# The mixing of a tree feed-forward on one Trainium2 core: twelve scaled copies of each block against one transposed block and path weights spread by TensorE

## The chip, the cores and the metric

The kernel runs on one core of one Trainium2 chip. The time is device microseconds of one execution; several executions of each kernel were timed, and one more was profiled. PE is TensorE, DVE is VectorE, ACT is ScalarE, POOL is GpSimd, and SP is SyncE, which here only issues DMAs.

## The reference, cut to what matters

The input x has shape 32 x 64 x 64 x 64. A tokenizer with small attention windows reduces it to 32 x 256 tokens of 64 features, a state space layer follows, and then a feed-forward in which each token walks down a binary tree of 8 levels. The change touches the last part and the rows that feed it.

```python
for _ in range(DEPTH + 1):                    # DEPTH = 7
    all_nodes.append(current)
    score = jnp.einsum('td,td->t', flat_x, w1s[current]) + b1s[current]
    all_logits.append(score)
    choice = ((jnp.sign(score) + 1.0) / 2.0).astype(jnp.int32)
    current = current * 2 + choice + 1
logits = jnp.stack(all_logits, axis=1)
path_weights = jax.nn.gelu(jnp.abs(logits), approximate=False)
out = jnp.zeros((T, OUTPUT_WIDTH), dtype=x.dtype)
for i in range(DEPTH + 1):
    nodes_i = all_nodes[i]
    t_i = jnp.einsum('td,tdo->to', flat_x, w2s[nodes_i]) + b2s[nodes_i]
    out = out + t_i * path_weights[:, i][:, None]
```

T is 8192 tokens. w2s holds 255 matrices of 64 x 64. All data is float32.

## The kernel before, in words

The program has three stages, one after the other: `tokenizer`, `scan_and_route` and `mix_blocks`. Between two stages every engine meets the others.

`scan_and_route` walks down the tree for all tokens and sorts them into 32 groups by their node at level 5. For each token it writes one row of `ROW` = 144 floats to DRAM (`rows_by_group`): the normalised token x (64 floats at `X0`), 12 path magnitudes (`P0`: six for levels 0 to 5, two candidates at level 6, four at level 7, zero where the token did not go), the token's h for the residual (64 at `H0`) and its number (`ID0`). POOL writes the rows with indirect DMAs, 8 of 128 rows for each of 8 chunks of 1024 tokens (`scatter`, L944), after computing some of the magnitudes (`path_weights`, L922 to L933).

`mix_blocks` takes the sorted rows in 96 blocks of 128 tokens; all tokens of a block belong to one group and need the same 14 matrices, stored as `wt`: 6 slabs of 128 x 64 (two units each) and a seventh slab with the biases and an identity that adds h. Two blocks, which the kernel calls h = 0 and 1, make a pair; there are 48 pairs.

- SP loads a block of rows into a ring of `ROWS` = 8 (L1579), once the block that lay there has been used.
- ACT applies gelu to the 24 magnitudes of a pair in place (L1630), copies the group's weights to `w_cur` (L1638), copies the four left turned slabs out of PSUM (L1640) and the results into `orow` (L1649), a ring of 8 blocks.
- DVE multiplies x by each of the 12 path weights, which makes `m_xs`, 12 scaled copies of 64 floats per token (L1600). It copies the other turned slabs (L1608) and the mixed result `oT` (L1614).
- PE transposes the 12 copies of a block, two at a time, and the magnitudes with h (L1666, L1671, L1673: 7 transposes a block). It then multiplies the 7 slabs of both blocks by the weights, the blocks in turn on the two column halves of the array (L1684: 14 matmuls, 28 records), and transposes the result back (L1691).
- POOL copies each block's token numbers to `ids` (L1701) and writes the result rows to `out` by indirect DMA (L1710).

Each engine's order is written out by hand. PE in step m turns pair m, mixes pair m - 1 and turns pair m - 2 back; steps of four pairs stand in a hardware loop. Each of `turned`, `mixed_bank` and `back_bank` exists twice in PSUM. So a product is turned back after the next pair's transposes and the next product have gone in between.

## Time and profile before

| | us |
|---|---|
| median of 3 runs | 756.32 |
| lowest, highest | 755.45, 758.33 |
| the profiled execution's own time | 755.77 |
| its span | 753.9 |
| tokenizer, until about | 352 |
| scan_and_route, until about | 545 |
| mix_blocks, from about 545 until its last DMA issue ends | 744.4 |

The profiled execution gives one span for the whole program; a row of the timeline starts with the time from the span's start and the length of the instruction, merged rows say x and a count, and the bracket tells how long the engine was idle before and what ended that. A releaser "remote" is one that the profile does not name. A PE record of a float32 matmul covers half of its passes, so 14 matmuls show as 28. PE's ends are modelled.

### The profile page before, as it was taken

To read this page: it belongs to the slowest core of one execution; us is meant where nothing else is said; L and a number is where in the kernel's file an instruction comes from. 1 tells how busy PE (TensorE), PEld (TensorE's weight loads), DVE (VectorE), ACT (ScalarE), POOL (GpSimd) and SP (SyncE) were. 2 spreads that over 40 slices of the span, in tenths; PEclk is the share of its full clock that TensorE was granted. 3 is DMA by queue.
4 is the path that set the end of the run, shared out by engine and by line. 5 is a ranking of instruction groups with operands and counts; after the bars stand their busy time and mean duration, and the time that the engine had idled before them with its cause. 6 is when DMAs were issued, how large, how long until landed. Compare 5 with 4: busy or idle time off the path is not lost. (4 is left out here: it accounts for less than half of the span.)

```text
span 753.9 us, 17120 instructions
## 1 busy us (share of the span) xinstructions
PE 634.7 (84%) x5322; PEld 333.0 (44%) x5322; DVE 564.2 (75%) x1090; ACT 451.2 (60%) x916; POOL 489.2 (65%) x541
## 2 busy tenths in 40 slices
PE   1699999999999999953799898873089999999990
PEld 1122222222222222211466565542078887887870
DVE  1379888888888889872489898987177777877770
ACT  1587777777777777611587777752055655656560
POOL 5756888888888887466105655557427776767773
PEclk9999999999999999985799999998579999999996
DMA  8033333333333330001776301001122222111200
GB/s 330 14 113 113 112 113 113 113 112 113 113 113 113 113 112 1 2 0 26 121 132 142 132 31 33 32 29 43 34 61 55 55 53 51 53 46 52 55 14 0
DMA packets 49055, 57.71 MB, mean 77 GB/s; under 512 B 31966, under 2 KB 44780, under 8 KB 46882
## 3 DMA queue, kind: packets, MB, share of 16 engines
q1 hardware_dynamic: 43410, 49.98, 22.2%
q0 software_dynamic: 5120, 6.84, 2.9%
q8 instruction: 31, 0.51, 0.3%
q14 instruction: 30, 0.25, 0.1%
q10 hardware_dynamic: 464, 0.13, 0.1%
HBM read 50.02 MB, written 10.28 MB: 80 GB/s over the span
## 5 line engine op out<-in xcount | busy, mean ns | idle before, releaser
L1710 POOL DMA_INDIRECT out<-orow,ids x96 | 100.3, 1044 | 60.0 <-DMA out<-orow,ids 33.5
L629 PE MATMUL b_v<-x_px,w_kv 64*64 64x512 f32 x256 | 133.3, 605 | 0.0
L630 PE MATMUL b_v<-x_px,w_kv 64*64 64x512 f32 x256 | 133.3, 605 | 0.0
L631 PE MATMUL b_k<-x_px,w_kv 64*64 64x512 f32 x256 | 133.3, 605 | 0.0
L628 PE MATMUL b_k<-x_px,w_kv 64*64 64x512 f32 x256 | 133.2, 604 | 0.0
L1600 DVE TENSOR_TENSOR m_xs<-m_rows 128x768 f32<-128x768 f32 x96 | 91.2, 950 | 26.5 <-ACT m_rows L1630 26.0
L399 POOL TENSOR_TENSOR pre<-va 128x1024 f32<-128x1024 f32 x32 | 76.2, 2382 | 41.8 <-DVE va L485 41.8
L944 POOL DMA_INDIRECT rows_by_group<-r_pay,r_slot_i x64 | 71.4, 1116 | 42.4 <-DVE r_slot_i L1295 24.7
L378 POOL TENSOR_TENSOR half_px<-x_px 128x1024 f32<-128x1024 f32 x32 | 75.9, 2372 | 32.3 <-DMA x_px<-in_x 27.0
L485 DVE TENSOR_TENSOR va<-b_a,v_sb 128x512 f32<-128x512 f32 x128 | 84.9, 685 | 12.5 <-PE b_a L646 12.4
L471 DVE TENSOR_TENSOR qk<-b_k,q 128x512 f32<-128x512 f32 x128 | 86.6, 679 | 8.2 <-PE b_k L631 6.8
L328 ACT ACTIVATE v_sb<-b_v 128x512 f32<-128x512 f32 x128 | 75.6, 591 | 24.7 <-PE b_k L631 23.7
L1684 PE MATMUL mixed_bank<-m_xsT,m_w_cur 128*64 128x128 f32 x1344 | 84.3, 276 | 0.8 <-ACT m_xsT L1640 0.8
L238 ACT ACTIVATE x_sq<-x_px 128x1024 f32<-128x1024 f32 x64 | 67.1, 1048 | 19.2 <-PE b_x L679 19.2
L1684 PEld LDWEIGHTS mixed_bank<-m_xsT,m_w_cur 128*64 128x64 f32 x1344 | 72.7, 137 | 9.4 <-issue 7.8
L643 PE MATMUL b_a<-a_sb,e_sw 64*64 64x512 f32 x128 | 68.8, 619 | 9.1 <-DVE va L485 9.1
L646 PE MATMUL b_a<-a_sb,e_sw 64*64 64x512 f32 x128 | 68.9, 619 | 0.0
L644 PE MATMUL b_a<-a_sb,e_sw 64*64 64x512 f32 x128 | 68.9, 619 | 0.0
L645 PE MATMUL b_a<-a_sb,e_sw 64*64 64x512 f32 x128 | 68.9, 619 | 0.0
L1638 ACT ACTIVATE m_w_cur<-wt 128x448 f32 x96 | 55.1, 574 | 18.1 <-issue 16.8
L628 PEld LDWEIGHTS b_k<-x_px,w_kv 64*64 64x64 f32 x256 | 29.0, 132 | 81.2 <-issue 62.0
L1666 PE MATMUL turned0a<-ident,m_xs 128*128 128x128 f32 x192 | 30.9, 285 | 20.7 <-DVE m_xs L1600 18.1
(235 smaller groups left out, 1621.7 us busy)
## 6 DMA issues: line engine op xcount, KB each, us to landing
x_px<-in_x SPq DMA_DIRECT2D x16, 2048.0 KB, 7.8
m_rows<-rows_by_group SPq DMA_DIRECT2D x96, 72.0 KB
wt<-in_w2T SPq DMA_DIRECT2D x8, 512.0 KB
rows_by_group<-rows_by_group SPq DMA_DIRECT2D x1, 2286.0 KB, 12.4
out<-orow,ids POOLq DMA_INDIRECT x96, 2.2
rows_by_group<-r_pay,r_slot_i POOLq DMA_INDIRECT x64
wt<-in_w2T SPq DMA_DIRECT2D x2, 256.0 KB
wt<-in_w2T SPq DMA_DIRECT2D x4, 128.0 KB
```

The costliest lines, as they stand in the source:

```text
L328: a.activation(v_sb[:, t % 2, n, :], b_v[n % 2][:, :], ACT.Copy).then_inc(done["v_copied"], 1)
L378: g.tensor_tensor(half_px[:, s, :, :], v[:, s, 0:2, :], v[:, s, 2:4, :], ALU.add).then_inc(done["px_halved"], 1)
L399: g.tensor_tensor(p1, v[:, :, 0:2, :], v[:, :, 2:4, :], ALU.add).then_inc(done["halved"], 1)
L471: d.tensor_tensor(qk[:, slot(n), :].rearrange("p (h s w) -> p h s w", s=S, w=HW), b_k[n % 2][:, :].rearrange("p (h s w) -> p h s w", s=S, ...
L485: d.tensor_tensor(va[:, slot(n), :], b_a[n % 2][:, :], v_sb[:, t % 2, n, :], ALU.mult).then_inc(done["va_ready"], 1)
L628: mm(b_k[i][LO, :], w_kv[LO, 0, LO], px(t, j, LO), start=True, stop=True)
L629: mm(b_v[i][HI, :], w_kv[LO, 1, LO], px(t, j, LO), start=True, stop=True)
L630: mm(b_v[i][LO, :], w_kv[HI, 1, HI], px(t, j, HI), start=True, stop=True)
L631: mm(b_k[i][HI, :], w_kv[HI, 0, HI], px(t, j, HI), start=True, stop=True).then_inc(done["kv_product"], 1)
L1600: d.tensor_tensor(xs[:, i % RING, :, :], rows[:, i, X0:X0 + C].rearrange("p (o c) -> p o c", o=1).broadcast_to([P, UNITS, C]), rows[:, i, ...
L1684: t = mm(ob[(j + 1) % 2][C * h:C * h + C, 0:P], w_cur[:, i + h, u, :], xsT[:, i + h, u, :], start=u == 0, stop=u == KT - 1)
L1710: nc.gpsimd.indirect_dma_start(out_d, bass.IndirectOffsetOnAxis(ap=ids[:, b % (2 * ROWS):b % (2 * ROWS) + 1], axis=0), orow[:, b % ROWS, : ...
```

## The change

The row becomes 208 floats: x is stored twice side by side (128 floats), so that one transpose of a block puts x on partitions 0 to 63 and again on 64 to 127. POOL makes the second copy once per chunk, ahead of the scatters.

In the mixing x is no longer multiplied before the transpose. ACT writes gelu of the magnitudes as bfloat16 and again as float32; DVE splits off two more bfloat16 parts, so that three parts add up to the float32 weight. PE transposes x, the magnitudes with h, and the parts. It then multiplies a constant 0/1 matrix (`unit_sel`) by the turned parts, which spreads each path weight over the 64 partitions of its unit: 6 products for each block, in two halves of 3 with PSUM banks and waits of their own. DVE multiplies the spread weights in PSUM by the turned x and writes the 6 slabs for the mixing to SBUF. Gelu and the split are done for 2, 2, 2, 2, 4, 4 and then 8 blocks at a time (`GROUPS`), some pairs ahead. The loop is written out, the rows' ring grows from 8 to 32 blocks and that of the results from 8 to 16, and POOL takes the token numbers straight from the rows. `turned_bank`, `mixed_bank` and `back_bank` exist once.

```diff
@@ -736,21 +736,21 @@
...
-ROW = 144
+ROW = 208
...
-X0, P0, H0, ID0 = 0, 64, 76, 140
+X0, P0, H0, ID0, K0 = 0, 128, 140, 204, 80
...
+        step(g.tensor_copy(ident_b[:, :], ident[:, :]))
+        step(g.memset(sel[:, :, :], 0.0))
+        v = sel[:, :, :].rearrange("p k (e c) -> p k e c", e=2)
+        for r in range(2):
+            for part in range(3):
+                step(g.affine_select(out=v, in_=v, compare_op=ALU.not_equal, fill=1.0, base=-(C * r + UNITS * part), pattern=[[-2, KT - 1], [-1, 2], [0, C]], channel_multiplier=1))
 
...
@@ -940,6 +946,8 @@
             pool.wait_ge(slots_ready, c + 1)
             pool.wait_ge(h_kept, 2 * c + 2)
             pool.wait_ge(x_kept, 2 * c + 2)
+            done(g.tensor_copy(pay[:, c % 2, :, X0 + C:X0 + 2 * C], pay[:, c % 2, :, X0:X0 + C]))
+            pool.wait_ge(weights, m[0])
             for k in range(QC):
                 g.indirect_dma_start(rows_d, bass.IndirectOffsetOnAxis(ap=slot_i[:, c % 2, k:k + 1], axis=0), pay[:, c % 2, k, :], None).then_inc(scattered[c % 2], 16)
...
+    PAIRS = NBLK // 2
+    RING, ORING, PARTS, TURNS = 32, 16, 16, 4
+    GROUPS = [(0, 2), (2, 4), (4, 6), (6, 8), (8, 12), (12, 16)] + [(b, b + 8) for b in range(16, NBLK, 8)]
...
+    rows = sb("m_rows", [P, RING, ROW])
+    rest = sb("m_rest", [P, PARTS, UNITS])
+    parts = sb("m_parts", [P, PARTS, C], BF16)
+    turns = sb("m_turns", [P, TURNS, 4, P])
+    partsT = sb("m_partsT", [P, 2, P], BF16)
+    xsT = sb("m_xsT", [P, 2, 2, 2, 3, P])
+    w_cur = sb("m_w_cur", [P, 4, KT, C])
...
+    orow = sb("orow", [P, ORING, C])
+    turned_bank, parts_bank = bank("turned_bank"), bank("parts_bank", (P, 1024), BF16)
+    spread_of = [bank(f"spread{f}", (P, 1024)) for f in range(2)]
+    mixed_bank, back_bank = bank("mixed_bank"), bank("back_bank")
...
+    def groups_at(t, wide, narrow):
+
+        return [n for n, (lo, hi) in enumerate(GROUPS) if lo // 2 - (wide if hi - lo == 8 else narrow + (lo >= 8)) == t]
...
     def _(sp):
...
+        for b in range(NBLK):
+            m = b // 2
+            if b >= RING and b % 2 == 0:
+                sp.wait_ge(*out_of(m - RING // 2))
+            r = sp.value_load(row0[0:1, b:b + 1], min_val=0, max_val=SPARE * BLK)
+            sp.dma_start(rows[:, b % RING, :], rows_d[bass.ds(r, BLK), :]).then_inc(in_of(m)[0], 16)
...
+        def remainder(n):
+            v.wait_ge(weighed, n + 1)
+            v.wait_ge(high, n + 1)
+            d.tensor_tensor(rest_of(n), weights_of(n), parts_of(n, 0), ALU.subtract).then_inc(split, 1)
+
+        def middle(n):
+            v.wait_ge(split, SPLIT["remainder", n])
+            d.tensor_copy(parts_of(n, 1), rest_of(n)).then_inc(split, 1)
+
+        def low(n):
+            v.wait_ge(split, SPLIT["middle", n])
+            d.tensor_tensor(parts_of(n, 2), rest_of(n), parts_of(n, 1), ALU.subtract).then_inc(split, 1)
+
+        def keep_parts(m):
+            v.wait_ge(turned, 2 * m + 2)
+            if m > 1:
+                v.wait_ge(spread, 2 * (m - 1))
+            d.tensor_copy(partsT[:, m % 2, :], parts_bank[:, 0:P]).then_inc(partsT_kept, 1)
+
+        def scale(m, f):
+            x = turns[:, m % TURNS, 0:2, :].rearrange("p (h o) n -> p h o n", o=1).broadcast_to([P, 2, 3, P])
+            w = spread_of[f][:, :].rearrange("p (h n) -> p h n", h=2)[:, :, 0:3 * P].rearrange("p h (k n) -> p h k n", k=3)
+            v.wait_ge(turns_kept, m + 1)
+            if m > 1:
                 v.wait_ge(mixed, m - 1)
...
+            v.wait_ge(spread, 2 * m + f + 1)
+            d.tensor_tensor(xsT[:, m % 2, :, f, :, :], w, x, ALU.mult).then_inc(scaled, 1)
+
+        def keep_mixed(m):
+            v.wait_ge(mixed, m + 1)
+            if m > 1:
+                v.wait_ge(back, m - 1)
+            d.tensor_copy(oT[:, m % 2, :], mixed_bank[:, 0:P]).then_inc(mixed_kept, 1)
+
+        for t in range(-1, PAIRS + 2):
+            if there(t):
+                keep_parts(t)
+            if there(t - 1):
+                scale(t - 1, 0)
+                scale(t - 1, 1)
+            if there(t - 2):
+                keep_mixed(t - 2)
+            for n in groups_at(t, 4, 1):
+                remainder(n)
+            for n in groups_at(t, 3, 1):
+                middle(n)
+            for n in groups_at(t, 2, 1):
+                low(n)
 
     @block.scalar
...
+        def weigh(n):
+            lo, hi = GROUPS[n]
+            for m in range(lo // 2, hi // 2):
+                act.wait_ge(*in_of(m))
+            if lo >= PARTS:
+                act.wait_ge(turned, lo - PARTS + hi - lo)
+            a.activation(parts_of(n, 0), weights_of(n), ACT.Gelu).then_inc(high, 1)
+            act.wait_ge(high, n + 1)
+            a.activation(weights_of(n), weights_of(n), ACT.Gelu).then_inc(weighed, 1)
+
+        def keep_turns(m):
+            act.wait_ge(turned, 2 * m + 2)
+            if m >= TURNS:
+                act.wait_ge(mixed, m - TURNS + 1)
+            a.activation(turns[:, m % TURNS, :, :].rearrange("p k n -> p (k n)"), turned_bank[:, :], ACT.Copy).then_inc(turns_kept, 1)
+
+        def keep_rows(m):
+            i = 2 * m % ORING
+            act.wait_ge(back, m + 1)
+            if 2 * m >= ORING:
+                act.wait_ge(*out_of(m - ORING // 2))
+            a.activation(orow[:, i:i + 2, :], back_bank[:, 0:P].rearrange("p (b c) -> p b c", b=2), ACT.Copy).then_inc(back_kept, 1)
+
+        def keep_weights(m):
+            if m > 1:
+                act.wait_ge(mixed, m - 1)
             for h in range(2):
...
+                g = act.value_load(gid[0:1, 2 * m + h:2 * m + h + 1], min_val=0, max_val=GRP - 1)
+                a.activation(w_cur[:, (2 * m + h) % 4, :, :], wt[:, bass.ds(g, 1), :, :].rearrange("p o k c -> p (o k) c"), ACT.Copy).then_inc(w_kept, 1)
+
+        act.wait_ge(zeroed, 1)
+        for t in range(-1, PAIRS + 3):
+            if there(t):
+                keep_turns(t)
+            if there(t - 3):
+                keep_rows(t - 3)
+            if there(t - 1):
+                keep_weights(t - 1)
+            for n in groups_at(t, 4, 1):
+                weigh(n)
 
...
+        def turn(m):
+            pe.wait_ge(split, SPLIT["low", GROUP_OF[2 * m]])
+            if m > 0:
+                pe.wait_ge(turns_kept, m)
+                pe.wait_ge(partsT_kept, m)
             for h in range(2):
...
+                nc.tensor.transpose(turned_bank[:, P * h:P * h + P], rows[:, (2 * m + h) % RING, X0:X0 + P], ident[:, :])
+            for h in range(2):
+                t = nc.tensor.transpose(turned_bank[:, P * (2 + h):P * (3 + h)], rows[:, (2 * m + h) % RING, K0:K0 + P], ident[:, :])
+            t.then_inc(turned, 1)
+            i = 2 * m % PARTS
+            nc.tensor.transpose(parts_bank[:, 0:P], parts[:, i:i + 2, :].rearrange("p b c -> p (b c)"), ident_b[:, :]).then_inc(turned, 1)
+
+        def spread_weights(m, f):
+            pe.wait_ge(partsT_kept, m + 1)
+            if m > 0:
+                pe.wait_ge(scaled, 2 * (m - 1) + f + 1)
+            for k in range(3):
+                for h in range(2):
+                    half = slice(C * h, C * h + C)
+                    t = mm(spread_of[f][:, 512 * h + P * k:512 * h + P * k + P], sel[half, 3 * f + k, :], partsT[half, m % 2, :], start=True, stop=True)
+            t.then_inc(spread, 1)
+
+        def mix(m, ks):
+            pe.wait_ge(scaled, 2 * m + 2)
+            pe.wait_ge(turns_kept, m + 1)
+            pe.wait_ge(w_kept, 2 * m + 2)
+            if m > 0:
+                pe.wait_ge(mixed_kept, m)
+            for k in ks:
+                for h in range(2):
+                    x = xsT[:, m % 2, h, k // 3, k % 3, :] if k < KT - 1 else turns[:, m % TURNS, 2 + h, :]
+                    t = mm(mixed_bank[C * h:C * h + C, 0:P], w_cur[:, (2 * m + h) % 4, k, :], x, start=k == 0, stop=k == KT - 1)
+            if KT - 1 in ks:
                 t.then_inc(mixed, 1)
...
+
+        def turn_back(m):
+            pe.wait_ge(mixed_kept, m + 1)
+            if m > 0:
+                pe.wait_ge(back_kept, m)
+            nc.tensor.transpose(back_bank[:, 0:P], oT[:, m % 2, :], ident[:, :]).then_inc(back, 1)
+
+        for t in range(PAIRS + 3):
+            if there(t - 0):
+                turn(t)
+            if there(t - 3):
+                turn_back(t - 3)
+            if there(t - 1):
+                spread_weights(t - 1, 0)
+            if there(t - 1):
+                spread_weights(t - 1, 1)
+            if there(t - 2):
+                mix(t - 2, range(KT))
 
...
+        nc.gpsimd.memset(parts[:, :, :], 0.0).then_inc(zeroed, 1)
         for b in range(NBLK):
...
+            m = b // 2
+            if b % 2 == 0:
+                pool.wait_ge(*in_of(m))
+                pool.wait_ge(back_kept, m + 1)
+            nc.gpsimd.indirect_dma_start(out_d, bass.IndirectOffsetOnAxis(ap=rows[:, b % RING, ID0:ID0 + 1].bitcast(I32), axis=0), orow[:, b % ORING, :], None,
+                                         bounds_check=TOKENS - 1, oob_is_err=False).then_inc(out_of(m)[0], 16)
...
```

How the rows of PE stand in the steady state before (the mixing's 14 products of L1684, the turns around them):

```order
L1684 MATMUL mixed_bank<-m_xsT,m_w_cur 64x128 x14
L1691 MATMUL back_bank<-ident,oT 128x128
L1666 MATMUL turned0a<-ident,m_xs 128x128 x4
L1671 MATMUL turned0b<-ident,m_xs 128x128 x2
L1673 MATMUL turned0b<-ident,m_rows 128x128
L1666 MATMUL turned1a<-ident,m_xs 128x128 x4
L1671 MATMUL turned1b<-ident,m_xs 128x128 x2
L1673 MATMUL turned1b<-ident,m_rows 128x128
```

and how they stand for one pair with the change:

```order
L1740 MATMUL mixed_bank<-m_xsT,m_w_cur 64x128 x12
L1740 MATMUL mixed_bank<-m_turns,m_w_cur 64x128 x2
L1714 MATMUL turned_bank<-ident,m_rows 128x128 x2
L1716 MATMUL turned_bank<-ident,m_rows 128x128 x2
L1719 MATMUL parts_bank<-ident_b,m_parts 128x128
L1748 MATMUL back_bank<-ident,oT 128x128
L1728 MATMUL spread<-m_partsT,unit_sel 128x128 x12
```

Fourteen transposes a pair have become five, and twelve products of 64 rows came in. The transpose back (L1748) now takes the product that was made just before the five turns; before, it took the one of a step earlier.

DVE in the steady state with the change, for two pairs:

```order
L1626 COPY m_partsT<-parts_bank 128x128
L1635 TENSOR_TENSOR m_xsT<-spread,m_turns 128x2x384 x2
L1641 COPY oT<-mixed_bank 128x128
L1612 TENSOR_TENSOR m_rest<-m_rows,m_parts 128x96
L1626 COPY m_partsT<-parts_bank 128x128
L1635 TENSOR_TENSOR m_xsT<-spread,m_turns 128x2x384 x2
L1641 COPY oT<-mixed_bank 128x128
L1616 CAST m_parts<-m_rest 128x8x12
```

The two multiplications of a pair stay in number and size; of DVE's copies out of PSUM the two of 384 columns are gone and one of 128 came in.

## Rows read from the trace of the kernel before

**Rows 1.** Windows of the mixing: us, each engine's busy time, clock, DMA share, GB/s
```profile
560.00:640.00 80.00, 77.96 (x914) 66.22 (x908) 60.67 (x104) 48.01 (x124) 55.74 (x81) 1.00 0.22 53
```

**Rows 2.** Timeline of PE, first pairs of the mixing: start, us, instruction
```profile
555.35 1.75 PE L1684 MATMUL mixed_bank<-m_xsT,m_w_cur 128*64 128x128 f32 x28
...
560.39 0.33 PE L1691 MATMUL back_bank<-ident,oT 128*128 128x128 f32 x1
...
563.85 0.33 PE L1691 MATMUL back_bank<-ident,oT 128*128 128x128 f32 x1
...
567.32 0.33 PE L1691 MATMUL back_bank<-ident,oT 128*128 128x128 f32 x1
```

**Rows 3.** Timeline of all engines, one pair in the middle of the mixing
```profile
642.42 1.75 PE L1684 MATMUL mixed_bank<-m_xsT,m_w_cur 128*64 128x128 f32 x28
...
644.42 0.98 POOL L1710 DMA_INDIRECT out<-orow,ids  x1 [0.16 <-issue]
...
646.08 0.29 DVE L1614 COPY oT<-mixed_bank 128x128 f32<-128x128 f32 x1 [1.40 <-remote]
646.26 0.28 ACT L1649 ACTIVATE orow<-back_bank 128x128 f32<-128x128 f32 x1 [2.65 <-remote]
...
647.39 1.27 POOL L1710 DMA_INDIRECT out<-orow,ids  x1 [1.79 <-DMA out<-orow,ids]
```

**Rows 4.** Groups of the mixing: count, busy us, mean ns, idle before and releasers
```profile
L1710 POOL DMA_INDIRECT out<-orow,ids x96 | 100.3, 1044 | 60.0 <-DMA out<-orow,ids 33.5 <-ACT orow L1649 15.9 <-issue 10.1
L1600 DVE TENSOR_TENSOR m_xs<-m_rows 128x768 f32<-128x768 f32 x96 | 91.2, 950 | 26.5 <-ACT m_rows L1630 26.0 <-PE turned0a L1666 0.4 <-PE turned1b L1673 0.2
...
L1640 ACT ACTIVATE m_xsT<-turned1a 128x512 f32<-128x512 f32 x48 | 28.3, 589 | 0.0
...
L1608 DVE COPY m_xsT<-turned0b 128x384 f32<-128x384 f32 x48 | 26.4, 550 | 0.0
...
L1614 DVE COPY oT<-mixed_bank 128x128 f32<-128x128 f32 x48 | 13.8, 287 | 37.2 <-remote 34.1 <-PE mixed_bank L1684 3.1
...
L1649 ACT ACTIVATE orow<-back_bank 128x128 f32<-128x128 f32 x48 | 13.3, 277 | 58.3 <-remote 51.7 <-PE back_bank L1691 6.6
```

**Rows 5.** Timeline of PE's weight loads: full width f32, bf16, two row halves
```profile
501.05 0.76 PEld L1383 LDWEIGHTS s_proj<-r_xn,r_w_p 64*128 64x128 f32 x8 [0.52 <-issue]
...
512.00 0.68 PEld L1489 LDWEIGHTS s_turn<-r_hot,r_one 128*128 128x128 bf16 x8
...
644.16 0.47 PEld L1666 LDWEIGHTS turned0a<-ident,m_xs 128*128 128x128 f32 x4
```

**Rows 6.** Timeline of POOL before the mixing
```profile
353.43 0.29 POOL L887 TENSOR_SCALAR_AFFINE_SELECT ident<-ident 128x128 f32<-128x128 f32 x1
...
358.38 2.12 POOL L902 TENSOR_SCALAR_AFFINE_SELECT wt<-wt 128x2048 f32<-128x2048 f32 x1
...
399.02 0.15 POOL L922 IOTA r_pay<- 128x8 int32 x1 [38.28 <-ACT r_pw L1099]
...
528.66 1.02 POOL L944 DMA_INDIRECT rows_by_group<-r_pay,r_slot_i  x1 [0.58 <-POOL r_pay L933]
```

**Rows 7.** Timeline of POOL at the start of the mixing
```profile
547.15 0.19 POOL L1701 COPY ids<-m_rows 128x1 int32<-128x1 int32 x1 [8.53 <-DMA m_rows<-rows_by_group]
...
550.42 0.18 POOL L1701 COPY ids<-m_rows 128x1 int32<-128x1 int32 x1 [0.84 <-DMA m_rows<-rows_by_group]
```

**Rows 8.** Timeline of the end of the mixing
```profile
734.26 1.75 PE L1684 MATMUL mixed_bank<-m_xsT,m_w_cur 128*64 128x128 f32 x28 [0.79 <-ACT m_xsT L1640]
...
738.41 0.29 DVE L1614 COPY oT<-mixed_bank 128x128 f32<-128x128 f32 x1 [4.86 <-remote]
738.44 0.28 ACT L1649 ACTIVATE orow<-back_bank 128x128 f32<-128x128 f32 x1 [4.07 <-remote]
...
739.57 0.97 POOL L1710 DMA_INDIRECT out<-orow,ids  x1 [2.07 <-ACT orow L1649]
...
743.40 0.97 POOL L1710 DMA_INDIRECT out<-orow,ids  x1 [0.30 <-issue]
```

More of the change, by code:

```diff
@@ L857, in _ @@
             r = GRP // cn
-            q = P0 - 16 + l
+            q = P0 - K0 + l
             ld(wt[q:q + 1, :, 6, :].rearrange("q (v r) o -> q v r o", r=r),
@@ new lines, in mix_blocks @@
+    w_cur = sb("m_w_cur", [P, 4, KT, C])
+    oT = sb("oT", [P, 2, P])
+    orow = sb("orow", [P, ORING, C])
+    turned_bank, parts_bank = bank("turned_bank"), bank("parts_bank", (P, 1024), BF16)
+    spread_of = [bank(f"spread{f}", (P, 1024)) for f in range(2)]
+    mixed_bank, back_bank = bank("mixed_bank"), bank("back_bank")
+    zeroed, weighed, high, split, turned, turns_kept, partsT_kept, spread, scaled, w_kept, mixed, mixed_kept, back, back_kept = (sem("m_" + n) for n in
+        "zeroed weighed high split turned turns_kept partsT_kept spread scaled w_kept mixed mixed_kept back back_kept".split())
@@ L1549, in mix_blocks @@
+    rows_in = [sem(f"m_rows_in{i}") for i in range(RING // 2)]
+    written = [sem(f"m_written{i}") for i in range(ORING // 2)]
     block = ctx.enter_context(nc.Block())
-    def due(n):
-        return not isinstance(n, int) or n > 0
     def there(m):
-        return not isinstance(m, int) or 0 <= m < PAIRS
-    def steps_of(eng, step, skew, ahead=0):
-        for m in range(-ahead, PEELED * TURN):
-            step(m // TURN, m % TURN)
-        with eng.Fori(PEELED, TURNS - ahead) as k:
-            for j in range(TURN):
-                step(k, j)
-        for m in range(PAIRS - TURN * ahead, PAIRS + skew):
-            step(m // TURN, m % TURN)
+        return 0 <= m < PAIRS
@@ new lines, in in_of, with out_of, weights_of, parts_of @@
+    def in_of(m):
+        return rows_in[m % (RING // 2)], 32 * (m // (RING // 2) + 1)
+    def out_of(m):
+        return written[m % (ORING // 2)], 32 * (m // (ORING // 2) + 1)
+    def weights_of(n):
+        lo, hi = GROUPS[n]
+        return rows[:, lo % RING:lo % RING + hi - lo, P0:P0 + UNITS]
+    def parts_of(n, s):
+        lo, hi = GROUPS[n]
+        return parts[:, lo % PARTS:lo % PARTS + hi - lo, UNITS * s:UNITS * s + UNITS]
+    def rest_of(n):
+        lo, hi = GROUPS[n]
+        return rest[:, lo % PARTS:lo % PARTS + hi - lo, :]
@@ L1569, in _ @@
+    def groups_at(t, wide, narrow):
+        return [n for n, (lo, hi) in enumerate(GROUPS) if lo // 2 - (wide if hi - lo == 8 else narrow + (lo >= 8)) == t]
+    SPLIT = {}
+    for t in range(-1, PAIRS):
+        for kind, wide in (("remainder", 4), ("middle", 3), ("low", 2)):
+            for n in groups_at(t, wide, 1):
+                SPLIT[kind, n] = len(SPLIT) + 1
     @block.sync
     def _(sp):
-        def load(k, i):
-            b = ROWS * k + i
-            if due(b - ROWS + 1):
-                sp.wait_ge(scaled, b - ROWS + 1)
-                sp.wait_ge(turned_b, b - ROWS + 1)
-                sp.wait_ge(ids_kept, b - ROWS + 1)
-            r = sp.value_load(row0[0:1, b:b + 1] if isinstance(b, int) else row0[0:1, bass.ds(b, 1)], min_val=0, max_val=SPARE * BLK)
-            sp.dma_start(rows[:, i, :], rows_d[bass.ds(r, BLK), :]).then_inc(rows_in[i], 16)
@@ L1580, in _ @@
-        for i in range(ROWS):
-            load(0, i)
-        with sp.Fori(1, TURNS) as k:
-            for i in range(ROWS):
-                load(k, i)
+        for b in range(NBLK):
[4 more added lines that the diff above has]
+            sp.dma_start(rows[:, b % RING, :], rows_d[bass.ds(r, BLK), :]).then_inc(in_of(m)[0], 16)
     @block.vector
@@ L1716, in program @@
+        for m in range(PAIRS - ORING // 2, PAIRS):
+            pool.wait_ge(*out_of(m))
 def program(nc, A, out):
```

128 lines of the change are left out of this document (12 added, 116 removed).

## The prediction

> **What bounds the kernel now.** I read the windows first, to see which stage the change touches and who is full there, then PE's timeline, then the groups with their idle time, then the timeline around a long idle gap. The change leaves the tokenizer alone, adds a little to the routing, and rewrites the mixing. There PE is busy 97% of the time from 560 to 640 us, DVE 76%, POOL 70%, ACT 60% [rows 1]. So PE looks like the bound. Its busy time hides something, though. At the start the products are turned back at 560.39, 563.85 and 567.32 us, 3.47 us a pair [rows 2]. The first product starts at 555.35 and the last, 47 pairs on, at 734.26 [rows 2, 8]: 3.81 us a pair. Counted from the fourth it is 3.83. So about 0.36 us a pair is lost to something other than PE's work.
>
> The groups show where. DVE's copy of the mixed product waited 34.1 us for a releaser that the profile does not name, and ACT's copy of the turned result 51.7 us [rows 4]. One such place reads as follows: PE starts a product of 28 records at 642.42 and should end it 1.75 us later, at 644.17. POOL issues a scatter from 644.42 to 645.40. DVE is idle, but takes the product only at 646.08, ACT follows at 646.26, and POOL's next scatter at 647.39 [rows 3]. At the very end DVE takes a product that PE should have ended at 736.01 only at 738.41 [rows 8]. So **a product's completion sometimes arrives some 2 us late**. It happens about every second pair, here with scatters going on. The kernel before bears it fairly well, because a product is turned back only one product later.
>
> **The change part by part.** The sum is made against the profiled execution, 755.77 us, which lies 0.55 under the median of 756.32; a measurement of this kernel can tell about 0.5% (3.8 us) from no change.
>
> PE, per pair. Nine transposes fewer: four full weight loads follow each other in 0.47 us less the last one's own length, 0.109 us each [rows 5], so -0.98. Twelve products of 64 rows by 128 columns in bfloat16 are new, and the trace has none like them. Eight bfloat16 loads of full width take 0.68 us, 0.085 each, with products of up to 256 columns between them; eight float32 loads on two row halves take 0.76 us, 0.095 each, for twice the columns and twice the passes, a quarter of which is 0.024 [rows 5]. That gives 1.02 us above and 0.29 below. I take 0.60, nearer the middle, since both halves of the rows take part but the loads are bfloat16 loads of full width. One more switch of shape (128 rows to 64 and on to the 64-column product) costs a gap like those around the product now: 3.47 less 14 transposes (1.53), 28 records at 0.054 (1.51) and a transpose back (0.11) leaves 0.32 for two, so +0.16. Together 3.47 - 0.98 + 0.60 + 0.16 = **3.25 us a pair** (2.94 to 3.67).
>
> Is PE still the bound? DVE loses two copies of 0.55 and keeps two multiplications of 0.95 (now 768 float32 from PSUM, the same count) and one copy of 0.29 [rows 4]; the copy of the turned parts (0.29 at most) and a quarter of three small steps (0.15) come in: 2.6 us. ACT loses one copy of 0.59, and POOL its copies of the token numbers; POOL then needs 1.28 us a scatter at the end's pace (739.57 to 743.40 in three steps [rows 8]), 2.56 a pair. All stay under 3.25, and I cost these edits at nothing; without PE as cover the next bound is DVE at 2.6. The larger ring of results removes no wait that I can see as due to the ring, so also nothing.
>
> The start. ACT runs gelu for blocks 16 to 23 before it copies pair 5 out of PSUM, so it waits for block 23. Blocks land 1.09 us apart (547.15 to 550.42 in three steps [rows 7]), a pace set by issuing, so I keep it for rows of 832 bytes in place of 576; block 23 lands at 547.15 + 23 x 1.09 = 572.2. Two gelus and a copy of 0.59 later PE can turn pair 6, at 573.4. By then the kernel before has turned back pair 4 and is turning pair 7. That loses a good pair.
>
> The routing. POOL's new copy of 512 floats is bounded by its selects: 0.29 us for 128 floats, 2.12 for 2048 [rows 6], so 0.66, and about 0.25 for the handing over. In the last chunk POOL waits only for itself (528.66 [rows 6]), and the chunk before runs straight into it, so two of the eight copies count: +1.8 us (0.9 to 7.3). Six selects of 768 and smaller constants, some 6.5 us, fall into POOL's idle 38.28 us before 399.02 [rows 6].
>
> The sum. PE turns pair 6 at 573.4 + 1.8 = 575.2, pair 47 after 41 P; two more steps, the first without turns (-0.66), and the last product alone (1.7) end at 576.3 + 43 P. From there to the end of the last scatter: completion 0.25, DVE 0.29, turn back 0.35, ACT 0.30, POOL's start 0.85 (739.57, less the end of the ACT copy that released it, 738.44 + 0.28), two scatters 2.25, together 4.3. With P = 3.25 that is 580.6 + 139.7 = 720.3. The last scatter now ends at 743.40 + 0.97 = 744.4 [rows 8]. So -24.1 us: 731.7 for the profiled execution, **732** for the median. My own range with this case, from P, is 719 to 750. Break-even is at P = 3.81.
>
> **The rivals.** *Completions stay as late as now* and cost 0.37 a pair: P = 3.62, 580.6 + 155.7 = 736.3, -8.1: **748**. For it: nothing in the change removes scatters. Against it: the kernel before lost nothing in its first three pairs [rows 2], though scatters had begun.
>
> *Completions late on every pair* is the rival on the other side. Now the transpose back stands right behind the five turns (0.6 us) that follow its own product, and DVE's copy (0.29) and a handing over already fill that. Each late completion then stops PE itself, and the turns and spread weights queued behind it, where before it had a whole product as slack. From 0.56 us a pair (3.81 - 3.25) it decides. At half of the 2 us seen [rows 3], P = 4.3: 580.6 + 184.9 = 765.5, +21.1: **777**. With nearly all of it on each pair, P = 4.8, it is 799. For it: POOL will be issuing 2.25 us of each pair, so most products end during a scatter. Against it: in the routing stage POOL scatters without a break and no wait there has this look, and at the start products passed.
>
> *The weight loads of the spreading are not hidden.* The bfloat16 loads in the trace are 0.085 apart with products of 256 columns and fewer between them [rows 5], so I can't see their own cost under 12 short products. If they cost a full-width float32 pair's 0.109 each, that is 1.31 us for twelve, P = 3.96: 580.6 + 170.3 = 750.9, +6.5: **763**. The Trainium skill, "TensorE: Matmul & The Clock Gate", section "LDWEIGHTS (loading the stationary operand)", says that a load takes its columns divided by 1.2 ns and that rows do not matter. By that rule, as an estimate, 128 columns take 107 ns and twelve 1.28 us, the same place. The trace's 0.085 speaks against it for bfloat16.
>
> **How the numbers follow.** The forecast 0.48; completions as late as now 0.15; late on every pair 0.24; loads not hidden 0.13. The first is faster but for a small tail at its upper bound, the second mostly faster; the other two are slower but for a small part within 0.5%. That makes faster 0.61, same 0.08, slower 0.31. The range must reach into the third case: from 720 (the lower bound of P, 719, has little behind it) to 785, which leaves out the worst of the late completions.
>
> **What would show it.** Starts of the products 3.25 us apart in the middle of the mixing; the twelve spreading products in about 0.6 us; DVE's idle time before its copy of the product named by PE, not "remote"; PE's first pairs paced by block 23's landing at about 574; two POOL copies of about 0.66 us ahead of the last scatters. The forecast is wrong if the products stand over 3.8 us apart, if DVE and ACT wait for a remote releaser in every pair, or if the spreading takes over 1 us.

## The result and the profile after

The changed kernel takes **780.34 us** (778.05 to 782.24), the kernel before 757.33 beside it (755.45 to 758.51): a ratio of 1.029, 95% interval 1.0249 to 1.0331. The forecast was 732. The span of the profiled execution is 780.5 us, 26.6 above the 753.9 of before, and it divides by three times that stand in the traces. The first product starts at 562.39 in place of 555.35 (+7.04); from the first to the last it is 202.54 in place of 178.91 (+23.63); from the start of the last product to the end of the span 15.6 in place of 19.7 (-4.1). Four executions of later sets stand far above the others of their kernel (739.99 us with before_few_scatters, 920.25 with after_scatter_by_8, 2145.19 and 3444.45 for the kernel before in experiment 2), and no ratio below uses them.

Windows of the changed kernel, in the columns of [rows 1]:

```profile
560.00:640.00 80.00, 63.80 (x832) 50.96 (x832) 43.37 (x94) 37.17 (x85) 33.36 (x34) 0.90 0.32 85
640.00:660.00 20.00, 16.21 (x205) 12.94 (x205) 11.04 (x23) 9.21 (x21) 7.85 (x8) 0.83 0.22 60
```

PE is busy 80% of the time where it was 97%, and its granted clock is no longer 1.00. No engine is full: something makes all of them wait. Groups of the mixing, the ones that answer to [rows 4]:

```profile
L1770 POOL DMA_INDIRECT out<-orow,m_rows x96 | 94.3, 982 | 128.1 <-ACT orow L1684 104.2 <-issue 23.9
L1635 DVE TENSOR_TENSOR m_xsT<-spread,m_turns 128x768 f32<-128x768 f32 x96 | 88.2, 953 | 41.1 <-remote 22.8 <-PE spread L1728 15.9 <-ACT m_turns L1677 0.9
...
L1677 ACT ACTIVATE m_turns<-turned_bank 128x512 f32<-128x512 f32 x48 | 28.6, 596 | 89.6 <-PE parts_bank L1719 72.2 <-remote 16.8 <-PE turned_bank L1716 0.3
...
L1641 DVE COPY oT<-mixed_bank 128x128 f32<-128x128 f32 x48 | 13.9, 289 | 32.8 <-PE mixed_bank L1740 22.7 <-remote 8.1 <-issue 2.1
```

The multiplication of the spread weights (L1635) costs what the one of before did, 953 ns, but it waits 22.8 us for a releaser that the profile does not name, and ACT's copy of the turned bank waits 16.8 us for one. The timeline of DVE, ACT, POOL and PE at one such place:

```profile
652.75 0.98 POOL L1770 DMA_INDIRECT out<-orow,m_rows  x1 [2.17 <-ACT orow L1684]
...
654.03 0.98 POOL L1770 DMA_INDIRECT out<-orow,m_rows  x1 [0.30 <-issue]
...
655.32 0.98 POOL L1770 DMA_INDIRECT out<-orow,m_rows  x1 [0.30 <-issue]
...
656.33 0.96 DVE L1635 TENSOR_TENSOR m_xsT<-spread,m_turns 128x768 f32<-128x768 f32 x1 [1.22 <-remote]
656.38 0.22 PE L1719 MATMUL parts_bank<-ident_b,m_parts 128*128 128x128 bf16 x1
656.60 0.98 POOL L1770 DMA_INDIRECT out<-orow,m_rows  x1 [0.30 <-issue]
658.63 0.29 DVE L1641 COPY oT<-mixed_bank 128x128 f32<-128x128 f32 x1 [1.34 <-remote]
658.72 0.60 ACT L1677 ACTIVATE m_turns<-turned_bank 128x512 f32<-128x512 f32 x1 [3.08 <-remote]
...
658.97 0.33 PE L1748 MATMUL back_bank<-ident,oT 128*128 128x128 f32 x1 [2.37 <-DVE oT L1641]
```

PE's last transpose ended at 656.60, and ACT takes it at 658.72. POOL scattered four blocks in a row, and its last scatter ended at 657.58. Now PE itself stands 2.37 us, because its next instruction waits for DVE's copy of the late product. That is what the second rival of the prediction describes. Where nothing is late PE's rows look like this, from the product of one pair to that of the next:

```profile
567.23 0.34 PEld L1728 LDWEIGHTS spread<-m_partsT,unit_sel 64*128 64x128 bf16 x12
567.24 0.51 PE L1728 MATMUL spread<-m_partsT,unit_sel 64*128 64x128 bf16 x12
567.67 1.53 PE L1740 MATMUL mixed_bank<-m_xsT,m_w_cur 128*64 128x128 f32 x24
...
569.36 0.44 PE L1714 MATMUL turned_bank<-ident,m_rows 128*128 128x128 f32 x2
...
569.90 0.28 PE L1748 MATMUL back_bank<-ident,oT 128*128 128x128 f32 x1
...
570.12 0.51 PE L1728 MATMUL spread<-m_partsT,unit_sel 64*128 64x128 bf16 x12
...
570.55 1.63 PE L1740 MATMUL mixed_bank<-m_xsT,m_w_cur 128*64 128x128 f32 x23
```

One pair takes 570.55 - 567.67 = **2.88 us** of PE, less than any value the prediction allowed. The products as a whole stand 202.54 / 47 = **4.31 us** apart, and 4.25 from the sixth on.

### The profile page after: what moved, and what is told of

The parts are those of the page before. It is cut to its first block and busy times, and to the rows that moved or that the text cites. A ratio compares the mean times of both kernels' runs of the same rounds, so it can differ in the third digit from the quotient of the medians.

```text
span 780.5 us, 16354 instructions
## 1 busy us (share of the span) xinstructions
PE 629.9 (81%) x5466; PEld 317.7 (41%) x5466; DVE 539.4 (69%) x1090; ACT 439.8 (56%) x851; POOL 465.9 (60%) x462
## 5 line engine op out<-in xcount | busy, mean ns | idle before, releaser
L1770 POOL DMA_INDIRECT out<-orow,m_rows x96 | 94.3, 982 | 128.1 <-ACT orow L1684 104.2
L1635 DVE TENSOR_TENSOR m_xsT<-spread,m_turns 128x768 f32<-128x768 f32 x96 | 88.2, 953 | 41.1 <-remote 22.8
L1677 ACT ACTIVATE m_turns<-turned_bank 128x512 f32<-128x512 f32 x48 | 28.6, 596 | 89.6 <-PE parts_bank L1719 72.2
L643 PE MATMUL b_a<-a_sb,e_sw 64*64 64x512 f32 x128 | 69.7, 626 | 8.9 <-DVE va L485 8.9
L645 PE MATMUL b_a<-a_sb,e_sw 64*64 64x512 f32 x128 | 69.8, 626 | 0.0
L644 PE MATMUL b_a<-a_sb,e_sw 64*64 64x512 f32 x128 | 69.8, 626 | 0.0
L646 PE MATMUL b_a<-a_sb,e_sw 64*64 64x512 f32 x128 | 69.8, 626 | 0.0
```

Source lines behind the costliest of these rows:

```text
L1635: d.tensor_tensor(xsT[:, m % 2, :, f, :, :], w, x, ALU.mult).then_inc(scaled, 1)
L1770: nc.gpsimd.indirect_dma_start(out_d, bass.IndirectOffsetOnAxis(ap=rows[:, b % RING, ID0:ID0 + 1].bitcast(I32), axis=0), orow[:, b % ORING ...
```

## The experiments

The kernels of one set ran on one chip, beside the same runs of the kernel before. Those runs turned out to matter: the kernel before took 732 to 733 us beside some sets of experiments and 757 to 759 beside others. I call them quiet and late runs; the change was measured in late ones.

**1. No scatters, plain writes, and scatters in longer runs.**

```diff
# after_few_scatters, before_few_scatters
+            if b < NBLK - ORING:    # before: NBLK - ROWS; waits for the missing writes left out
+                continue
             nc.gpsimd.indirect_dma_start(out_d, ...
# after_plain_writes, on SP's queue
+                sp.dma_start(out_d[at:at + BLK, :], orow[:, b % ORING, :])
# after_scatter_by_8, POOL
             if b % 2 == 0:
...
-                pool.wait_ge(back_kept, m + 1)
+            if b % 8 == 0:
+                pool.wait_ge(back_kept, m + 4)
```

> The changed kernel, its result rows scattered only for the last 16 of 96 blocks; 80 blocks are computed and not written (left out). Theory A (a scatter holds PE's completions back until it has landed, and PE stands): between the scatters the products follow each other every 2.88 us, as in its four undisturbed places, so the mixing takes 47 x 2.9 = 136 us in place of 202.5 and the whole about 780 - 66 = 714 us; no idle time with a remote releaser and full clock in the middle. Theory B (the chain over single PSUM banks is too tight by itself, whatever POOL does): products 4.2 to 4.4 us apart, 770 us or more. Theory C (the clock alone): 20 us of half speed less at most, 760 us.

> The kernel before, with result rows scattered only for the last 8 of 96 blocks (88 are not written). Theory A: products 3.47 us apart as in its first pairs, not 3.83, so 47 x 0.36 = 17 us less: 740 us, and no remote releaser. Theory B: unchanged, 756.

> The changed kernel, its result rows written by plain DMAs from SP's queue, block after block and so to wrong places, in place of POOL's indirect DMAs. The bytes and the time at which they are written stay. Theory A1 (POOL's issuing of an indirect DMA, or its landing packets on that queue, holds the completions): 714 us as without scatters. Theory A2 (any write of results to DRAM does): 775 to 785 us. Theory B: 770 us or more.

> The changed kernel, POOL waits until four pairs are in the results' ring and then scatters their 8 blocks in one run, 1.28 us apart; nothing else moves. Theory A with one hold per run of scatters: one long hold in place of two, between 750 and 770 us. Theory A with a hold as long as the run (10 us of each 17): slower, 790 us or more. Theory B: 780 us, plus some 4 us at the end, where 8 scatters wait for the last pair.

The kernel before took 733.04 beside them, 24 us less than in the runs of record. Measured: 717.44, 726.12, 723.91 and 730.85 (ratio of the last 0.9968, 0.9948 to 0.9987). The products were 2.88 us apart in the first and in the last, scatters or not, and 3.47 in the second; in the third five gaps were 3.9 to 5.5 us, where ACT waited up to 3.2 us for the load of a block. So the 717 us near theory A's 714 prove nothing: with scatters in runs of 8 nothing was late either, and that run came out 19 us under all three of its expected cases. In none of the four traces does an engine wait for a remote releaser in the mixing. These four couldn't tell the theories apart; what they say is that lateness depends on something outside the kernel.

**2. The two kernels as they are.**

> The changed kernel as it is. The kernel before took 733 us in the runs of the last four, 24 us less than where the change was measured, and this one has no time beside it yet. If scatters hold completions in the same way there: products 4.1 to 4.3 us apart, 755 to 765 us, 3% slower than before. If the holds are shorter or fewer on that chip: below 745 us.

> The kernel before as it is, for its profile on the chip of these runs: with few scatters its products stood 3.47 us apart throughout and it took 726 us. Theory A: the same lateness as in the first profile, only shorter or rarer: products 3.55 to 3.65 us apart, 731 to 736 us.

Measured: the changed kernel **721.74**, the kernel before 731.30 without its two far executions (732.14 with them); ratio 0.9869, 0.9841 to 0.9896. The profiled execution of before_again took 733.13. Here the change makes the kernel faster. The groups of the changed kernel in this run:

```profile
L1635 DVE TENSOR_TENSOR m_xsT<-spread,m_turns 128x768 f32<-128x768 f32 x96 | 87.4, 952 | 13.8 <-PE spread L1728 13.8
...
L1641 DVE COPY oT<-mixed_bank 128x128 f32<-128x128 f32 x48 | 14.0, 291 | 4.8 <-PE mixed_bank L1740 4.8
```

No releaser is "remote" any more. The products are 2.88 us apart from the sixth on (3.47 in the kernel before, where 3.55 to 3.65 was expected). From the first to the last it is 143.93 us (161.29 in before_again), 58.6 us less than in the late run; the same difference for the kernel before is 17.6. So in the mixing the lateness costs the changed kernel three times what it costs the one before. Over the whole execution it is 780.34 - 721.74 = 58.6 against 757.33 - 731.30 = 26.0, and those 33 us turn a gain of 1.3% into a loss of 2.9%.

**3. The transpose back behind the spreading.** PE's turn_back(t - 3) was moved behind the two calls of spread_weights.

> The changed kernel with PE's transpose back moved behind the 12 spreading products. The product's completion gets 0.5 us more before PE stands. Theory A: held completions of 2 us still stop the chain in the turns, the spreading and the one bank of the product: within 5 us of the unchanged one. Theory D (it is the place of the transpose back alone that costs, as the prediction's rival put it): 15 us or more faster than the unchanged one.

Measured 727.29 in the same quiet set, 5.5 us slower than after_again, which neither theory expected: products 3.02 us apart. Its place before the spreading is the better one when nothing is late. Whether it helps against late completions isn't shown by a quiet run; theory D stays untested.

**4. A smoother start.**

```diff
-    GROUPS = [..., (12, 16)] + [(b, b + 8) for b in range(16, NBLK, 8)]
+    GROUPS = [..., (12, 16)] + [(b, b + 4) for b in range(16, 32, 4)] + [(b, b + 8) for b in range(32, NBLK, 8)]
```

> Scatters in runs of 8 as before, and the gelu groups of blocks 16 to 31 made 4 blocks wide, so that ACT no longer waits for block 23 before it empties the turned bank. In the last run with 8-wide groups the fourth product was followed by 7.99 us and the fifth by 4.86 (half clock), against 2.88 later on. If the wide group is the cause, both come to about 2.9 to 3.5: 5 to 7 us less than the 730.9 of that run, 724 to 726 us. If the loads' pace is the limit anyway: 729 to 731.

Measured 724.63, as expected, again with runs of 8 scatters. The gaps after the fourth and fifth product went from 7.99 and 4.86 us in after_scatter_by_8 to 3.00 and 2.88, and the last product starts at 699.86 in place of 706.33 in after_again. The wide group was the cause. The 8 scatters that then remain take the gain away: from the last product to the end it is 23.1 us, and 15.6 in after_again. I didn't run the small groups alone with scatters in twos.

**5. The decisive set, in late runs.** start_early has these groups, with those of blocks 2 to 15 one pair earlier. In two of its variants something is left out: "few scatters" writes the last 16 of 96 blocks only, "plain writes" writes to other places.

> The changed kernel with a smoother start: blocks 16 to 31 in gelu groups of 4, and the groups of blocks 2 to 15 taken one pair earlier. Scatters as in the change. If the kernel before takes some 732 us beside it (a chip without late completions): the 8.2 and 4.65 us after the fourth and fifth product become about 2.9 each and the first two some 1 us less, 721.7 - 7 to 8 = 714 us. If the kernel before takes some 756 us (a chip with late completions): products 4.2 us apart behind the start, 770 to 778 us.

> The same with scatters for the last 16 of 96 blocks only (80 left out). Kernel before at 732: products 2.88 us apart with or without scatters, within 3 us of start_early. Kernel before at 756: theory A says 2.88 us apart here too, 50 us or more below start_early; theory B (the chain is tight whatever POOL does) says within 10 us of it.

> The same as start_early with scatters in runs of 8. Kernel before at 732: 5 us above start_early, since 8 scatters wait for the last pair, not 2 to 4. Kernel before at 756: if a hold costs once for each run of scatters, 735 to 755 us; if it lasts as long as POOL issues, 780 or more.

> The same as start_early with the result rows written by plain DMAs from SP's queue to wrong places, no indirect DMA. Kernel before at 732: no nearer than the same 714 to 720 us. Kernel before at 756: theory A1 (POOL's indirect DMAs hold the completions) says 2.9 us apart, 720 us; theory A2 (any write of results) says 4.2 us apart, 770 us.

| beside the kernel before at 758.62 | us | ratio, interval |
|---|---|---|
| start_early | 774.65 | 1.0215, 1.017 to 1.0261 |
| few scatters | 719.65 | 0.9487, 0.945 to 0.9524 |
| scatters by 8 | 837.69 | 1.103, 1.0992 to 1.1069 |
| plain writes | 728.34 | 0.9601, 0.9562 to 0.964 |

Theory A holds and B falls: without the scatters of 80 blocks 55 us go, and the products are 2.88 us apart. The last 16 blocks of that run show both cases in one trace. POOL's first scatter starts at 687.30, and from there on completions are late again; the next products stand 5.30, 4.50, 2.88 and 5.20 us apart:

```profile
687.30 1.00 POOL L1769 DMA_INDIRECT out<-orow,m_rows  x1 [138.40 <-ACT orow L1681]
688.61 0.99 POOL L1769 DMA_INDIRECT out<-orow,m_rows  x1 [0.30 <-issue]
...
690.91 1.82 DVE L1638 TENSOR_TENSOR m_xsT<-spread,m_turns 128x768 f32<-128x768 f32 x2 [2.18 <-remote]
```

Plain DMAs of the same bytes from SP's queue hold nothing: no wait of that mixing has a remote releaser. Their 728 us, where theory A expected 720, come from single gaps of 3.4 to 6.9 us; at the longest ACT waits 3.95 us for the load of a block, as in the quiet run of experiment 1. And a hold does last as long as POOL scatters. Runs of 8, behind which no completion was late in the quiet set, cost 63 us here. Windows 600 to 680 us of start_early_few_scatters:

```profile
600.00:680.00 80.00, 79.92 (x1274) 68.40 (x1272) 66.15 (x133) 55.83 (x125) 0.00 (x0) 1.00 0.29 73
```

and of start_early_by_8:

```profile
600.00:680.00 80.00, 54.33 (x662) 42.14 (x661) 34.63 (x71) 30.50 (x67) 31.40 (x32) 0.79 0.20 52
```

PE falls from full to 68%, and its clock to a mean of 0.79. One run of 8 scatters of start_early_by_8 in its timeline:

```profile
645.63 0.98 POOL L1770 DMA_INDIRECT out<-orow,m_rows  x1 [11.52 <-ACT orow L1683]
...
646.92 0.98 POOL L1770 DMA_INDIRECT out<-orow,m_rows  x1 [0.30 <-issue]
...
649.29 0.96 DVE L1638 TENSOR_TENSOR m_xsT<-spread,m_turns 128x768 f32<-128x768 f32 x1 [2.09 <-remote]
...
651.32 0.38 PE L1713 MATMUL turned_bank<-ident,m_rows 128*128 128x128 f32 x2 [0.98 <-issue]
...
652.75 0.38 PE L1715 MATMUL turned_bank<-ident,m_rows 128*128 128x128 f32 x2 [1.05 <-issue]
652.87 0.96 DVE L1638 TENSOR_TENSOR m_xsT<-spread,m_turns 128x768 f32<-128x768 f32 x1 [2.62 <-remote]
...
654.63 0.98 POOL L1770 DMA_INDIRECT out<-orow,m_rows  x1 [0.30 <-issue]
657.23 0.29 DVE L1644 COPY oT<-mixed_bank 128x128 f32<-128x128 f32 x1 [3.40 <-remote]
657.32 0.60 ACT L1676 ACTIVATE m_turns<-turned_bank 128x512 f32<-128x512 f32 x1 [7.77 <-remote]
```

The first scatter alone holds nothing. From the second on, completions trickle: one at 649.2, one at 652.8, all others 1.6 us after the last scatter's end at 655.61. PE's own rows stand apart too ("issue" of about 1 us between two transposes that have nothing to wait for). So it isn't only the signal that seems late; PE's stream itself hardly moves. (PE's ends are modelled, so the trace can't say how much of a hold is the signal's and how much PE's own.)

start_early as such was no gain: 774.65 is within a few us of what the change took (1.0215 against 1.029, intervals that overlap). Its earlier groups bring the first product to 11.2 us behind the first load of the mixing, where the change has 13.8 (558.52 in this trace), but ACT then waits for blocks that have not landed; in the quiet run "spaced" below, with the same groups, 3.73 us before a gelu and a gap of 6.81 us after the fourth product.

**6. Which part of a scatter, and what distance does.** Two pieces of POOL's code:

```diff
# scatter_skipped: all but row 0 out of bounds
-                                         bounds_check=TOKENS - 1, oob_is_err=False)
+                                         bounds_check=0, oob_is_err=False)
# pool_plain
+            nc.gpsimd.dma_start(out_d[at:at + BLK, :], orow[:, b % ORING, :])
...
# before_spaced (in "spaced": scaled, min(2 * m + 6, NBLK))
+            if b % 2:
+                pool.wait_ge(kept_a, min(b + 7, NBLK))
```

> The kernel before; POOL's second scatter of each pair waits also for ACT's copy a of three pairs on, so that the two scatters of a pair stand about 1.7 us apart in place of 1.3. Where the kernel before takes 732: no change, 731 to 735. Where it takes 757: if only scatters less than some 1.5 us apart hold completions, products 3.5 us apart and about 740 us; if any succession does, 755 to 760.

> start_early, POOL's second scatter of each pair waits also for DVE's second multiplication two pairs on: scatters about 1.5 and 1.4 us apart at full pace. Kernel before at 732: 714 to 722. Kernel before at 757: start_early took 774.7 beside it; if distance helps in part, 745 to 765; if only a distance over 1.5 us does, 770 to 780.

> start_early with the bound of the scatters at 0, so that POOL makes its descriptors for all rows and nearly none is written (the output rows are left out). Kernel before at 757: if making the descriptors holds completions, 765 to 780 as start_early; if the landing rows do, 715 to 725. Kernel before at 732: no difference, 712 to 720.

> start_early with plain DMAs from POOL's queue to wrong places in place of the indirect ones. Kernel before at 757: if POOL's own making of descriptors of any kind holds completions, over 760; if only indirect ones do, 715 to 730. Kernel before at 732: 712 to 725.

These ran quiet (732.0): 731.61, 717.87, 718.92 and 714.65, each within its range for 732, so they tell nothing of the lateness. "spaced" is the fastest complete kernel that I ran: 0.9806 (0.9758 to 0.9853) of the kernel before, against 0.9869 for the change; the two intervals overlap. Whether plain DMAs from POOL hold completions stays open. Two of them were run again and met late runs (757.78 beside them):

> As before_spaced. Where the kernel before takes 757: if only scatters less than some 1.5 us apart hold completions, products 3.5 us apart and about 740 us; if any succession does, 755 to 760. Where it takes 732: 731.6 again.

> As scatter_skipped. Kernel before at 757: if making the descriptors holds completions, 765 to 780 as start_early; if the landing rows do, 715 to 725. Kernel before at 732: 718.9 again.

scatter_skipped_2 took **773.69** (1.0217, 1.0181 to 1.0253), as start_early with real scatters in its own late set. Its DMA queues, 560 to 770 us, first the queue's packets, MB and share:

```profile
q0 software_dynamic: 3072, 0.06, 1.1%
```

start_early moved 2.12 MB there. The packets are as many, 3072 in both. So nearly no row lands and all is as late as before: it's **POOL's making of the descriptors**, or what the queue does with them apart from the rows, and not the landing of data. No run takes these two apart. The Trainium skill, "DMA: Bandwidth & Descriptors", section "SWDGE vs HWDGE vs iDMA", says that DMAs issued from GpSimd have their descriptors computed by it and written into rings in SBUF, and those from SP or ACT do not. The runs agree as far as they go: indirect DMAs from POOL hold completions (774.65 us), and DMAs from SP's queue don't (728.34). The page says nothing of completions that are held.

before_spaced_2 took **749.35**, 0.9898 (0.9881 to 0.9916) of the kernel before: between the two expectations. Its scatters up to pair 33 stand like this, and the products start 3.47 us apart (3.56 at most):

```profile
620.86 0.98 POOL L1712 DMA_INDIRECT out<-orow,ids  x1 [0.88 <-ACT orow L1649]
...
622.38 0.98 POOL L1712 DMA_INDIRECT out<-orow,ids  x1 [0.16 <-issue]
...
624.46 0.98 POOL L1712 DMA_INDIRECT out<-orow,ids  x1 [0.90 <-DMA out<-orow,ids]
...
625.84 0.98 POOL L1712 DMA_INDIRECT out<-orow,ids  x1 [0.15 <-issue]
```

Later POOL falls behind and catches up with three in a row:

```profile
683.10 0.98 POOL L1712 DMA_INDIRECT out<-orow,ids  x1 [0.16 <-issue]
...
684.44 0.98 POOL L1712 DMA_INDIRECT out<-orow,ids  x1 [0.16 <-issue]
...
685.77 0.98 POOL L1712 DMA_INDIRECT out<-orow,ids  x1 [0.16 <-issue]
...
687.42 0.29 DVE L1614 COPY oT<-mixed_bank 128x128 f32<-128x128 f32 x1 [2.72 <-remote]
```

Pairs of scatters 1.4 to 1.5 us apart, with 2.1 us from the second to the next pair's first, cost PE nothing at first. But they are not free: DVE takes the first product 0.05 us after its end and the 32nd 1.12 us after it; in the quiet before_spaced it is never more than 0.35 us from the 16th to the 44th. Three scatters with 1.33 us between them hold the product until 0.67 us after the last one's end, and the products are 5.2 to 5.4 us apart there, every third pair. Distance and number change together here, so the run doesn't say which of them decides. "spaced" met no late set, and whether distance helps the changed kernel stays open.

## Why the prediction was wrong, point by point

**The step that failed** is the wait that the sum put at nothing. P = 3.25 starts from 3.47 us a pair, the pace without lateness, and has no term for late completions, though the traced pace was 3.81; their return on every pair got 0.24 against 0.48. From the sixth product on the runs show 4.25 us a pair: 2.88 of PE's own work and 1.37 on top of it. The 1.37 go when the scatters go (2.88 in start_early_few_scatters, on the kernel with the earlier groups). [rows 3] showed the lateness, [rows 4] its 34.1 and 51.7 us, and nothing in the change took scatters away. I should have kept it as given, and asked only who stands behind a late completion.

Both reasons against the lateness were misread. "In the routing stage POOL scatters without a break and no wait there has this look" is false. The same trace has three waits of 3.3 to 3.4 us for a remote releaser there, all of ACT for a product that PE should have ended 2.5 us before. This is the first of them, and below it the same place in before_again:

```profile
450.97 0.60 PE L1476 MATMUL s_logits<-r_b,r_pick 64*128 64x256 f32 x4
...
452.30 0.99 POOL L944 DMA_INDIRECT rows_by_group<-r_pay,r_slot_i  x1 [0.30 <-issue]
454.09 0.60 ACT L1087 ACTIVATE r_lg<-s_logits 128x512 f32<-128x512 f32 x1 [3.36 <-remote]
```

```profile
452.30 0.60 ACT L1087 ACTIVATE r_lg<-s_logits 128x512 f32<-128x512 f32 x1 [0.88 <-PE s_logits L1476]
```

Every late trace has such waits in the routing, and no quiet one has. "At the start products passed" is true of three. DVE took the fourth product at 568.72, 1.33 us after its end and behind four scatters in a row, where before_again has 0.05. The kernel's slack hid it.

**The rival's price** came near by luck. It had P = 4.3 and 777 us, measured 4.25 and 780. But it takes 3.25 for the work, 0.37 too much, and some 1.0 for the lateness, 0.3 to 0.4 too little.

**Why it costs three times as much.** In the kernel before a product is turned back one product later, its banks are double, and it loses 17.6 us (late against quiet). The change has one turned bank, one product bank and one bank back, and the turns, the spreading and the multiplication of one pair each hand over within 2.88 us. Held completions stop PE itself, results then come in bunches, and POOL scatters the bunches in runs of two and four. That bunching lengthens the next hold; this last link is argued from the timelines and from the runs by 8, not tested alone.

**The clock.** In the late run it fell eight times between 575 and 760 us; the windows above show means of 0.90 and 0.83, while the kernel before kept 1.00 [rows 1]. That is TensorE's lower level of 1.2 GHz for 3.4 to 6.8 us each time, in or behind a pair that had taken 5.6 to 6.8 us. The eight stretches are 37.5 us together; half of that, 18.8 us, is the most that half the clock can have cost, of the 58.6. The waits bring it about, as far as the runs show: in start_early_few_scatters the clock stays at 1.00 from 600 to 680 us. The prediction had no term for it.

**PE's work** was forecast at 3.25 us a pair (2.94 to 3.67) and is 2.88. The transposes went as counted (five take 569.90 - 569.36 = 0.54 us). The twelve spreading products take 567.67 - 567.24 = 0.43 us, not 0.60, and the extra switch (+0.16) doesn't show: 3.47 - 0.98 + 0.43 = 2.92. The rival "loads not hidden" falls with it: the row of PEld above has the twelve loads at 0.34 us together. By the rule of the Trainium skill that the prediction cites, twelve loads would be 1.28 us, an estimate. The trace disagrees, and it decides.

**The start** went as described and later than priced. ACT waits for block 23, and PE turns pair 6 at 578.40, forecast 575.2. Of the 3.2 us 1.7 come from the routing below, and the rest is mostly a later landing of block 23.

```profile
576.78 0.28 ACT L1669 ACTIVATE m_parts<-m_rows 128x96 bf16<-128x96 f32 x1 [2.84 <-DMA m_rows<-rows_by_group]
...
578.40 0.41 PE L1714 MATMUL turned_bank<-ident,m_rows 128*128 128x128 f32 x2 [2.02 <-DVE m_partsT L1626]
```

The first product also runs at the lower clock, which lasts until 565.3 (554.9 in the kernel before): the second stands 5.28 us behind it, 3.36 before.

**The routing** was priced at +1.8 us for POOL's copies. A copy takes 0.61, as forecast (0.66). But the first load of the mixing starts 3.53 us later (548.71 for 545.18), and 6.9 later in the quiet pair (548.75 for 541.86). From POOL's first scatter to that load it is 140.0 us in the kernel before and 140.3 in the changed one in the late pair, 134.2 and 140.9 in the quiet pair. So the change costs 6.7 us there, and the late completions had cost the kernel before nearly as much. The rest of the 3.53 lies ahead of the first scatter (408.40 for 405.16), where the two kernels' runs differ by that much among themselves. The missing term is most likely the wider row in its DMAs; no run changes it alone. Nearly all of the 6.9 us falls into one place: from POOL's first scatter of the second chunk to that of the third it is 23.9 us in after_again and 17.8 in before_again. The DMA that clears the rows grew, as the issues of before_again and after_again show (KB, us to landing):

```profile
rows_by_group<-rows_by_group SPq DMA_DIRECT2D x1, 2286.0 KB, 9.6
```

```profile
rows_by_group<-rows_by_group SPq DMA_DIRECT2D x1, 3302.0 KB, 13.0
```

POOL's first scatters go out beside it, and ACT waits until they have landed to reuse their buffer, in the late run and in after_again, where the trace of the kernel before has at most 1.3 us for this:

```profile
430.44 0.38 ACT L1076 ACTIVATE r_pay<-s_turn 128x256 f32<-128x256 f32 x1 [3.41 <-DMA rows_by_group<-r_pay,r_slot_i]
```

```profile
430.58 0.38 ACT L1076 ACTIVATE r_pay<-s_turn 128x256 f32<-128x256 f32 x1 [5.18 <-DMA rows_by_group<-r_pay,r_slot_i]
```

The change's step listed the row's 832 bytes and costed them only in the mixing's loads.

**The end** was priced at 1.7 + 4.3 = 6.0 us from the last product to the last scatter's end, and is 771.01 - 764.93 = 6.1.

**In quiet runs** the forecast's case is what one sees: products paced by PE, and 721.74 - 731.30 = -9.6 us. That it isn't -24 is because the kernel before has no lateness to lose there either (it runs at 3.43 us a pair, not 3.81), and because the first product starts 10.5 us later (562.40 for 551.85), most of it the routing's 6.9.

## What to carry to other kernels

Count the waits whose releaser the profile cannot name before touching the slack behind them. Here the chain with single buffers paid 58.6 us for delays of which the looser one paid 17.6, so work taken off the full engine made the kernel slower. Look for such waits in every stage: the routing had them too. Price a wider row in every DMA that carries it, the clearing of the buffer included.

## What the runs showed that I had not expected

PE's completions can be held, and its own instructions set about 1 us apart, while POOL issues indirect DMAs back to back (1.28 us apart), mostly until 0.5 to 1.8 us after the last; whether the rows land makes no difference. It is present in some sets of runs and absent in others with the same kernels: 732 or 758 us for the kernel before, 721.7 or 780.3 for the changed one, within 1% inside each set, the far executions aside. One chip showed both. What decides it between sets stays open. Whoever measures such a kernel needs the reference beside it in the same set, and more than one set.
